# A routed expert stage: expert numbers loaded four at once, gates carried with the rows

## What is computed

```
logits = einsum('btd,ed->bte', x, Wr)                 # 8 experts
probs = softmax(logits)
topk_vals, topk_idx = top_k(probs, 2)
router_weights = topk_vals / topk_vals.sum(-1, keepdims=True)
gate = the two weights, each at its expert's place, 0 elsewhere
h = silu(einsum('btd,efd->btef', x, W1))              # 512 wide
y = einsum('btef,edf->bted', h, W2)
out = einsum('bte,bted->btd', gate, y)
```

## Time and profile before

| | |
|---|---|
| runs | 582.85, 584.41, 586.38 us |
| profiled execution, first to last instruction (span) | 580.7 us |
| TensorE busy | 483.9 us (83%) |
| VectorE, ScalarE, GpSimd busy | 306.7, 243.7, 247.1 us |
| mean granted TensorE clock | 0.891 |
| expert stages | about 273 to 391 us and 463 to 581 us of the span |

### The profile page before, as it was taken

The page is one execution under the profiler, slowest core; times in us unless marked ns, Lnnn a source line. Parts: engine busy times, 40 slices in busy tenths (PEclk is TensorE's granted clock), DMA queues, the critical chain, the costliest instruction groups (busy, mean ns, idle before and its releaser), DMA issues.

```text
span 580.7 us, 12462 instructions
## 1 busy us (share of the span) xinstructions
PE 483.9 (83%) x4005; PEld 383.5 (66%) x4027; DVE 306.7 (53%) x1012; ACT 243.7 (42%) x507; POOL 247.1 (43%) x229
## 2 busy tenths in 40 slices
PE   1879999999989999888799999907997499999960
PEld 0546776768666887585797787705777388787750
DVE  5676496858876898445740110055867743010116
ACT  7735566574547443604223232315764033232330
POOL 7143363335332655540547443520217536643450
PEclk9959899999989996968679999956999579999995
DMA  7882293985669183010022310040001222331007
GB/s 241 247 164 44 62 165 90 138 157 76 131 95 174 25 156 57 14 52 19 29 70 70 99 47 23 35 145 1 1 2 48 61 61 61 94 80 31 25 24 217
DMA packets 66593, 48.35 MB, mean 83 GB/s; under 512 B 7861, under 2 KB 60615, under 8 KB 66534
## 3 DMA queue, kind: packets, MB, share of 16 engines
q1 hardware_dynamic: 61430, 36.99, 31.0%
q0 software_dynamic: 5104, 10.57, 5.2%
HBM read 16.14 MB, written 27.59 MB: 75 GB/s over the span
## 4 chain that ended last, share of the span: by engine, by line
PE 67%; DVE 12%; issue 7%; SPq 5%; POOL 3%; DMA 3%; ACT 2%; DVEq 0%; POOLq 0%
PE PS L806 13%; PE PS L651 9%; PE PS L790 7%; PE PS L792 4%; SPq L303 4%; PE PS L638 3%; PE PS L791 3%; PE PS L613 3%; PE PS L701 3%; PE PS L554 2%; PE PS L661 2%; POOL XS L494 2%; PE PS L595 2%; PE PS L622 2%; PE PS L632 2%
## 5 line engine op out<-in xcount | busy, mean ns | idle before, releaser
L506 POOL DMA_INDIRECT YY<-W2R,ID x78 | 76.8, 985 | 84.0 <-ACT W2R L1263 65.4
L450 POOL TENSOR_TENSOR R<-NM,I64B 128x1024 bf16<-128x1024 f32 x32 | 61.6, 1924 | 109.1 <-DVE NM L1425 104.1
L1255 ACT ACTIVATE W2R<-PS 128x512 f32<-128x512 f32 x78 | 46.6, 597 | 121.2 <-PE PS L792 121.2
L806 PE MATMUL PS<-WB,W2R 128*128 x624 | 90.9, 291 | 0.1
L790 PE MATMUL PS<-QKM,WA 128*128 128x128 bf16 x312 | 73.2, 236 | 10.5 <-issue 4.3
L806 PEld LDWEIGHTS PS<-WB,W2R 128*128 128x128 f32 x624 | 78.1, 197 | 2.4 <-issue 0.3
L494 POOL DMA_INDIRECT XS<-W1R,SLOT x64 | 63.6, 994 | 37.0 <-DVE SLOT L1551 20.0
L1698 DVE COPY QKM<-PS 128x1024 bf16<-128x1024 bf16 (+1 forms) x20 | 13.5, 677 | 123.2 <-PE PS L769 123.2
L792 PE MATMUL PS<-QKM,WA 128*128 128x128 bf16 x312 | 73.2, 236 | 0.0
L791 PE MATMUL PS<-QKM,WA 128*128 128x128 bf16 x312 | 71.1, 229 | 0.0
L651 PEld LDWEIGHTS PS<-VB,PF 128*128 128x128 f32 x512 | 62.8, 201 | 8.6 <-issue 8.6
(11 more groups left out here) (207 smaller groups left out, 875.7 us busy)
## 6 DMA issues: line engine op xcount, KB each, us to landing
XS<-CST SPq DMA_DIRECT2D x30, 520.0 KB, 10.1
QKM<-XS SPq DMA_DIRECT2D x78, 65.0 KB
QKM<-QK SPq DMA_DIRECT2D x64, 72.0 KB, 2.1
QKM<-YY SPq DMA_DIRECT2D x16, 256.0 KB, 5.0
W2R<-in_W POOLq DMA_DIRECT2D x1, 2048.0 KB, 11.2
YY<-W2R,ID POOLq DMA_INDIRECT x78, 2.2
XS<-CST SPq DMA_DIRECT2D x2, 585.0 KB, 10.8
XS<-W1R,SLOT POOLq DMA_INDIRECT x64, 2.4
```

Source lines behind the costliest of these rows:

```text
L450: nc.gpsimd.tensor_tensor(R[:, u % 2], NM[:, u % 2].unsqueeze(2).to_broadcast([P, NH, WIN]), I64B[:].unsqueeze(1).to_broadcast([P, NH, WIN ...
L506: pool.indirect_dma_start(out=YY[f], out_offset=to, in_=YS[n % NY][:, i, :], in_offset=None, bounds_check=NPAIRS - 1, oob_is_err=False) \
L806: last = mm(o, HF[n % 3][:, k, :], WB[:, e, k, :].rearrange("p o c -> p (o c)"), start=k == 0, stop=k == KF - 1)
L1255: fn(HF[n % 3], PS[:, n % 3, :].rearrange("p (k s) -> p k s", k=KF), ACT.Silu).then_inc(s["f_hf"], 1)
```

## The change

*Expert numbers.* TensorE loads the numbers of a group's tiles in one call, once per group, with the check of their range left out.

*Gates.* A row carries one more word: the difference of the second-best logit to the best. ScalarE takes tanh of half of it when a group's rows have come, VectorE turns it into the gate (0.5 plus or minus half of the tanh, by whether the row is a first or a second choice), and `y_out` copies each tile by itself, with the gate as the scale of its rows. Exp, `route_gates` and the multiplications in `combine` go; two additions of 128x256 take their place in each half. Waits follow: SP refills a buffer only when the gate of its last group is made, GpSimd counts tiles copied instead of groups.

```diff
-XROW = D + 2
+XROW = D + 3
...
+                        sp.wait_ge(s["f_gate"], n - 2)
...
-                    pool.wait_ge(s["f_ys"], n + 1)
+                    pool.wait_ge(s["f_ys"], f * NTILE + tiles[-1] + 1)
...
-                def choose(t):
+                def choose(g):
+                    tiles = GROUPS[g]
                     for i, (_, t0, _) in enumerate(PHASES):
-                        if t == t0:
+                        if tiles[0] == t0:
                             pe.wait_ge(s["f_table"], 2 * (NPH * f + i + 1))
-                    which[t] = pe.value_load(EID[0:1, t:t + 1], min_val=0, max_val=NE - 1)
+                    _, values = nc.values_load_multi_w_load_instructions(
+                        EID[0:1, tiles[0]:tiles[-1] + 1], [mybir.EngineType.PE], min_val=0, max_val=NE - 1,
+                        skip_runtime_bounds_check_because="a count of eight comparisons, at least 1, less 1")
+                    which.update(zip(tiles, values))
...
-                    if t + 1 < NTILE:
-                        choose(t + 1)
+                    if t + 1 < NTILE and (t + 1) % 4 == 0:
+                        choose((t + 1) // 4)
...
+                def tanh(g):
+
+                    n, ts = f * NGRP + g, slice(GROUPS[g][0], GROUPS[g][-1] + 1)
+                    act.wait_ge(s[f"f_xg{n % 3}"], 16 * x_got(f, g))
+                    if f:
+                        act.wait_ge(s["f_gate"], NGRP)
+                    fn(TANH[:, ts], XG[n % 3][:, 0:len(GROUPS[g]), D + 2], ACT.Tanh, scale=0.5).then_inc(s["f_tanh"], 1)
+
                 def y_out(y):
                     m = f * len(YGROUPS) + y
-                    w = len(YGROUPS[y])
                     act.wait_ge(s["f_y"], f * NTILE + YGROUPS[y][-1] + 1)
+                    act.wait_ge(s["f_gate"], f * NGRP + YGROUPS[y][-1] // 4 + 1)
                     if m >= NY:
                         act.wait_ge(s[f"f_ysent{m % NY}"], 16 * y_sent(m % NY, f, y - NY + 1))
-                    fn(YS[m % NY][:, 0:w, :], PS[:, 4 + m % 2, 0:w * D].rearrange("p (t d) -> p t d", d=D), ACT.Copy) \
-                        .then_inc(s["f_ys"], 1)
+                    for i, t in enumerate(YGROUPS[y]):
+                        fn(YS[m % NY][:, i, :], PS[:, 4 + m % 2, i * D:i * D + D], ACT.Copy, scale=GATE[:, t:t + 1]) \
+                            .then_inc(s["f_ys"], 1)
 
                 if f:
                     route_x_t(f, B - 1)
+                tanh(0)
                 for t in range(NTILE):
                     silu(t)
+                    if t % 4 == 2 and t // 4 + 1 < NGRP:
+                        tanh(t // 4 + 1)
...
-                act.wait_ge(s["f_lg"], (f + 1) * B)
-                fn(PRE, PR, ACT.Exp).then_inc(s["f_exp"], 1)
...
-                fs.did(v.tensor_reduce(GS[:, 1, js], REST[:, js], op=ALU.max, axis=AXX))
+                fs.did(v.tensor_reduce(XD[:, js, D + 2], REST[:, js], op=ALU.max, axis=AXX))
...
-            def route_gates(f):
...
                     v.tensor_tensor(ID[:, ts], NEQ[:, ts], XG[n % 3][:, 0:w, D], ALU.add).then_inc(s["f_id"], 1)
+                    dve.wait_ge(s["f_tanh"], n + 1)
+                    fs.did(v.scalar_tensor_tensor(HALF[:, ts], NEQ[:, ts], 0.5, TANH[:, ts], ALU.subtract, ALU.mult))
+                    fs.settle()
+                    v.tensor_scalar(GATE[:, ts], HALF[:, ts], 0.5, None, ALU.add).then_inc(s["f_gate"], 1)
...
                     dve.wait_ge(s[f"f_yl{2 * c + h}"], 16 * (f + 1))
+                    xs = X[:, TB * c + 2 * h:TB * c + 2 * h + 2, :]
+                    first, second = (YL[c][:, 2 * h:2 * h + 2, k, :] for k in range(TOP_K))
+                    fs.did(v.tensor_tensor(xs, xs, first, ALU.add))
                     fs.settle()
-                    for k in range(TOP_K):
-                        for j in (2 * h, 2 * h + 1):
-                            t = TB * c + j
-                            last = v.scalar_tensor_tensor(X[:, t, :], YL[c][:, j, k, :], GK[:, k, t:t + 1], X[:, t, :],
-                                                          ALU.mult, ALU.add)
-                            if k == 0:
-                                fs.did(last)
-                        fs.settle()
-                    last.then_inc(s["f_x"], 1)
+                    v.tensor_tensor(xs, xs, second, ALU.add).then_inc(s["f_x"], 1)
```

More of the change, by code:

```diff
@@ L221, in program @@
         many = most * NE
-        PR, PRE, REST, SE, VV = (vb[:, one * i:one * i + one].rearrange("p (t e) -> p t e", e=NE) for i in range(5))
+        PR, REST, SE, VV = (vb[:, one * i:one * i + one].rearrange("p (t e) -> p t e", e=NE) for i in range(4))
         CAND, TOP, SEL = (vb[:, one * i:one * (i + 2)].rearrange("p (k t e) -> p k t e", k=TOP_K, e=NE)
-                          for i in (5, 7, 9))
-        GT, GW = (vb[:, 11 * one + many * i:11 * one + many * (i + 1)].rearrange("p (t e) -> p t e", e=NE)
+                          for i in (4, 6, 8))
+        GT, GW = (vb[:, 10 * one + many * i:10 * one + many * (i + 1)].rearrange("p (t e) -> p t e", e=NE)
                   for i in range(2))
-        GS, GK = sb("GS", [P, 4, NT]), sb("GK", [P, TOP_K, NT])
+        GS, GK = sb("GS", [P, 2, NT]), sb("GK", [P, TOP_K, NT])
         MB = sb("MB", [P, B, TB * NE], BF16)
@@ L232, in program @@
         USED0 = sb("USED0", [P, 1])
-        small = 11 * one + 2 * many
+        small = 10 * one + 2 * many
         OE, NEQ = (vb[:, small + NTILE * i:small + NTILE * (i + 1)] for i in range(2))
@@ L237, in program @@
         ID = sb("ID", [P, NTILE], I32)
+        TANH, HALF, GATE = (sb(n, [P, NTILE]) for n in ("TANH", "HALF", "GATE"))
         XS = [nc.dram_tensor(f"XS{f}", (CAP * NE + P, XROW), F32, kind="Internal").ap() for f in range(2)]
@@ L272, in program @@
             "a_ht", "a_h_ps", "a_h1", "a_y_ps", "a_x",
-            "f_steps", "f_xz", "f_xt_ps", "f_ft", "f_lg_ps", "f_lg", "f_m", "f_rk_ps", "f_rk", "f_slot", "f_exp", "f_table",
+            "f_steps", "f_xz", "f_xt_ps", "f_ft", "f_lg_ps", "f_lg", "f_m", "f_rk_ps", "f_rk", "f_slot", "f_tanh", "f_gate", "f_table",
             "a_var", "a_rstd", "f_var", "f_rstd", "b_var", "b_rstd", "b_nmr", "pad0", "pad1", "xd_ready", "f_sent0", "f_sent1", "f_sent2", "f_xg0", "f_xg1", "f_xg2",
@@ L801, in outputs @@
                     if t == YGROUPS[y][0] and m >= 2:
-                        pe.wait_ge(s["f_ys"], m - 1)
+                        h, before = divmod(m - 2, len(YGROUPS))
+                        pe.wait_ge(s["f_ys"], h * NTILE + YGROUPS[before][-1] + 1)
                     i = t - YGROUPS[y][0]
@@ L1520, in route_choose @@
                 fs.settle()
-                fs.did(v.tensor_reduce(GS[:, 1, js], REST[:, js], op=ALU.max, axis=AXX))
+                fs.did(v.tensor_reduce(XD[:, js, D + 2], REST[:, js], op=ALU.max, axis=AXX))
                 fs.settle()
-                fs.did(v.tensor_tensor(SE[:, js], REST[:, js], each(GS[:, 1, js]), ALU.is_equal))
+                fs.did(v.tensor_tensor(SE[:, js], REST[:, js], each(XD[:, js, D + 2]), ALU.is_equal))
                 fs.settle()
@@ L1526, in route_choose @@
                 fs.settle()
-                fs.did(v.tensor_reduce(GS[:, 2, js], CAND[:, 1, js], op=ALU.max, axis=AXX))
+                fs.did(v.tensor_reduce(GS[:, 1, js], CAND[:, 1, js], op=ALU.max, axis=AXX))
                 fs.settle()
-                fs.did(v.tensor_tensor(TOP[:, 1, js], CAND[:, 1, js], each(GS[:, 2, js]), ALU.is_equal))
+                fs.did(v.tensor_tensor(TOP[:, 1, js], CAND[:, 1, js], each(GS[:, 1, js]), ALU.is_equal))
                 fs.settle()
@@ L1742, in experts @@
                     identities(g)
-                route_gates(f)
             def combine(f, c):
```

11 lines of the change are left out of this document (removed).

## The result

The changed kernel took **557.75 us** (median of four runs, 549.36 to 559.09) beside 583.72 us of the kernel before on the same chip (582.85 to 586.38): a ratio of 0.948, 95% interval 0.940 to 0.956. Run again later, against other runs of before, the ratio was 0.962 (0.955 to 0.970).

The account below looks back on a forecast made before the run. The prediction took TensorE's sequencer to bound the expert loops. Its terms, -21.6 + 6.8 - 0.3 + 0.6 - 2.8 = -17.3 us, took the median from 584.41 to 567 us, range 557 to 579.

Parts of the forecast that it names:

- the big term: Expert loops, tiles 16 to 37: four expert numbers per load save 10.8 us per stage, -21.6 in both.
- the rival of four loads' price: Expert-number loads: a load of four costs four single loads, 1.43 us instead of 0.36, giving 578 us; chance 0.20.
- The nearer one: Expert-number loads: at some 200 ns per register, a load of four takes 0.9 us, giving 572 us; no separate chance.
- what that standing costs: Behind TensorE's stand before tile 16: 8 us at half clock cost 3.4 us per stage, +6.8.
- ahead of tile 16: First scaled copy, ahead of the dispatches: tile 16 +0.6 us in the first stage, -0.9 in the second, together -0.3.
- combining: Adding expert results: two additions per half replace multiply-adds, 1.7 us at the end and 1.1 after the first stage, -2.8.
- closing copies: Last two-tile group's scaled copy, opening the closing scatters: +0.3 us per stage, +0.6.
- Four scaled copies: ScalarE's copies out of PSUM: four cost 1.0 to 1.5 us, 1.2 taken, 0.6 more than one copy.
- tanh: ScalarE, ten per stage: covered by two tiles, 3.8 us, even if table swaps made it 2.9 us.
- Hidden loads: Expert loops: something else holds a tile at 2.41 us, so no pace is gained, 583 us; chance 0.08.
- Half clock that stays: Behind tile 16 in both stages: the clock does not come back, costing 19 us per stage, 620 us; chance 0.06.
- The clock that holds: Stand before tile 16: it is shorter or the clock returns at once, so 6.8 us go unpaid, 560 us; chance 0.14.

Follow-up runs that it names:

- (1): The kernel before with only the loads of four expert numbers added, gates and combining as before: 551.16 us, ratio 0.946.
- (3): The changed kernel with one expert number loaded per tile, still without comparison and assertion: 565.19 us, ratio 0.962.
- (4): The changed kernel with four expert numbers loaded at once, but each compared and asserted: 559.56 us, ratio 0.967.
- (6): The changed kernel with 72 dummy matmuls added at tile 15, in TensorE's stand ahead of tile 16: median 553.17 us.
- (5): The changed kernel with GpSimd dispatching the last chunk ahead of the first group's result scatters: 546.18 us, ratio 0.953.
- before again: A second profile of the kernel before, with no edit: 300.9 us from first tile to end.
- (7): The changed kernel with combining as multiply-adds of 128x128 again, by a constant 1.0: 558.9 us, ratio 0.967.
- (2): The changed kernel with expert numbers loaded one per tile and checked again, leaving gates and combining new: 577.61 us, ratio 0.985.

## Why the prediction was right, and where it was wrong

**Right: the bound and the big term.** The expert loops were held by TensorE's sequencer, and the load with its comparison was the block that held them: (1), (3) and (4) show it. The load of four cost 0.33 us, the low end of 0.36 to 1.43 and the value taken. That refutes the rival of four loads' price. The nearer one, by the Trainium skill (Runtime: NRT & Kernel Launch, Instruction fetch mechanics), has some 200 ns for each register even in bulk, a figure of the registers that the runtime loads; it doesn't carry over to these loads from `EID`, where 332 ns for four are 83 each.

At full clock (6) a stage's tiles 16 to 37 take 39.15 instead of 50.65, 11.5 where 10.8 was forecast. The difference is the tile's pace: 39.15 / 21 = 1.86 instead of 1.90, or 1.84 by the 38.6 of (5).

**Wrong: the term "what that standing costs", +6.8.** The stand came, 4.2 us for some 4 foretold, and half clock came behind it. The price of a tile at half clock was right as well: tile 16 to tile 17 took 324.25 - 321.16 = 3.09 for 3.3. Wrong was the overlap. The prediction took 8 us of half clock from the earlier trace rows and laid all of them on tiles behind tile 16. After, 6 us follow the restart, and 2.65 of these are gone before tile 16 starts, on transposes and the outputs of tile 13. Some 3.3 us are left, the first layer of tile 16 and the outputs of tile 14. At the prediction's own rate these are 3.3 x (1 - 1.90 / 3.3) = 1.4 in a stage, and 1.2 is what the first stage shows without dummies (6).

The 8 us were a misreading as well. Of the two restarts in the earlier trace rows the second doesn't give a length of half clock behind a stand: the clock of the kernel before was at 0.50 already from 448 to 464 us, ahead of it, with TensorE busy for 7.32 of these 16 us.

```profile
448.00:464.00 16.00, 7.32 (x40) 6.18 (x39) 12.49 (x57) 1.46 (x3) 9.23 (x10) 0.50 0.18 52
```

With the clock held (6), tiles 16 to 37 gain 0.8 and 0.4 where the prediction charged 3.4 and 3.4, and the stretch ahead of tile 16 gains another 0.5 and 0.6: **2.3 in all instead of 6.8**, net of what the dummies themselves cost. From the transposes to tile 17 alone it is 2.2 in a stage; even taken whole, 4.4, that is less than was charged.

The sum, from the first tile on and against before again: tiles 16 to 37 -14.8 forecast, -21.7 measured (6.9 of the error: by (6) 5.6 clock and 1.3 pace); ahead of tile 16 -0.3 forecast, +0.1 measured; behind tile 37 with combining and closing copies -2.2 forecast, -3.4 measured; the second attention +1.1, which is an execution's and not the change's, since (5) has the same change and 70.6 there. That is -17.3 forecast and -23.9 measured.

The other 6 of the 13 us between 567 and 554 belong to no term of the sum: from the first tile on, -23.9 would make 584.4 into 560.5, inside the range. They lie in the executions that the ratio compares, and what makes them up is not shown. (The -2.8 of combining is rounded down: ten halves by 0.30 are 3.0.)

**A smaller omission: tiles 37 and 38.** The prediction counted the saved loads to tile 37 and not beyond. The loads of four alone shorten the way from tile 37 on by 0.6 in the first stage (22.2 to 21.6) and by 0.4 in the second (25.5 to 25.1), 1.0 together; that is most of the 1.2 missed there.

**Right, and small.** Combining: 2.8, by (7), of which 1.6 at the end are clean and 1.2 a net. Four scaled copies: 1.14 for 1.2. Ahead of tile 16 dispatch sets the end: (5) moves it, by 0.9 us in the first stage and by 6.4 in the second. tanh: covered, and without any swap. The Trainium skill (ScalarE: Activation LUTs, Table sets: the hidden batching unit) places tanh with exp and with sigmoid and does not place Silu; here tanh ran between Silus with no table load, so the 2.9 us that the prediction priced for a swap never arose. The Exp table was loaded where ScalarE then still waited 1.41 us for VectorE, so it cost nothing, as said.

**The rivals.** Hidden loads: refuted by (1). Half clock that stays: it was back after 6 us. The clock that holds, 560, was the nearest: the stand and the fall came, against its condition, but they cost little, as it supposed. That 560.5 meets its number is partly luck: what the half clock did cost and the 1.1 of the second attention cancel the gains of the pace and of tiles 37 and 38.

**What the gates part is worth.** The loads alone (1) took 551.16 us, the whole change again 552.56, and from the first tile on 276.1 and 277.2. By itself the gates part gains 1.7 us (2); beside the loads nothing that these runs can tell. What is gained behind tile 37 (21.6 to 20.7 and 25.1 to 23.7) is lost in tiles 16 to 37 (38.5 to 39.8 and 39.0 to 39.6), which fits the half clock that ends later there (3.3 and 3.0 us behind tile 16 instead of 0.7 and 1.2), and ahead of tile 16.

## What to carry to other kernels

Where an engine's instructions have hardly any gaps and yet no tile is as fast as one behind a backlog, look at its sequencer: here a register load between instructions cost its 0.30 us per tile and a comparison with its assertion 0.27, and one load for four values cost little more than one for one. When a clock falls behind a stand, lay its duration on the timeline from the restart on and price only what really runs in it, not a stage's average tiles. When a stretch gets faster, ask at once what feeds its start: here a one-line change of GpSimd's order was worth another 7 us ahead of tile 16 and 6 of the median. A run that fills a stand with dummy work doesn't price the clock alone: here the stand also ended later in each of the three stages that had dummies.

## What the runs showed that was not expected

- A load of four words into registers took 332 ns, of one 302.
- A range comparison with its assertion cost 0.27 us per tile of sequencer time, nearly as much as the load itself, though its records add up to 0.164.
- Where half clock ends differs by some 3 us between kernels whose stands are 3.2 to 4.2 us. In the first stage it ended 3.3 us behind the start of tile 16 in both profiles of the changed kernel, and within 0.3 us of that start where the results left in one copy and where the last dispatch came first. What sets this was not tried. A stand of 1.9 us ahead of the same transposes in (3) had a clock of 1.00 in the 6 us behind it.
